# An attention and FP4-FFN layer on one core: the quantisation of the FFN weights is taken apart and its pieces are placed in the second pass

## The reference

```
xn   = (x - mean) / sqrt(var + 1e-5)
attn: q = xn @ Wqa @ Wqb (16 heads of 8), kv = xn @ Wkva @ Wkvb (4 kv heads of 8)
      rope on q and k, causal softmax(q k^T / sqrt(8)) v, @ Wout + bout
ffn:  gate = fp4(xn) @ fp4(w_gate)^T,  up = fp4(xn) @ fp4(w_up)^T     (352 hidden)
      h = silu(gate) * up,  out = fp4(h) @ fp4(w_down)^T
out  = x + attn + ffn
```

## Time and profile before

| | |
|---|---|
| runs (median) | 821.9 us |
| profiled execution | 822.47 us, its span 820.7 us, mean granted clock 0.969 |
| busy: PE, DVE, ACT, POOL | 91%, 78%, 67%, 73% of the span |
| chain that ended last | PE 73%, DVE 8%, ACT 6%, POOL 4%, SyncE's queue 3% |
| PEclk, 40 slices | `9668799999999999999999999999999999999997` |

### The profile page before, as it was taken

How to read it: one execution, slowest core, us unless ns; L and a number is a source line. 1 busy time by engine, 2 the same in 40 slices (tenths; PEclk the granted TensorE clock), 3 DMA queues, 4 the chain that set the end, 5 groups by cost and what they waited for, 6 DMA issues and landing times.

```text
span 820.7 us, 18663 instructions
## 1 busy us (share of the span) xinstructions
PE 746.0 (91%) x6641; PEld 468.1 (57%) x6733; DVE 637.2 (78%) x1396; ACT 553.2 (67%) x1169; POOL 602.6 (73%) x706
## 2 busy tenths in 40 slices
PE   2277899999999999999999999999999999999886
PEld 1143455665657565665756566666656565656444
DVE  4479788888788888888788888888887888787310
ACT  1213586777777777777777777777777777776771
POOL 5324597878879797878788797878788797856561
PEclk9668799999999999999999999999999999999997
DMA  4412323141314233241414232241413232230000
GB/s 115 124 48 77 78 75 80 54 107 50 86 45 112 58 93 76 58 111 45 98 36 109 53 105 64 63 106 50 111 49 84 47 97 60 81 75 9 21 15 14
DMA packets 66518, 58.24 MB, mean 71 GB/s; under 512 B 17554, under 2 KB 56434, under 8 KB 66426
## 3 DMA queue, kind: packets, MB, share of 16 engines
q1 hardware_dynamic: 66426, 57.04, 27.0%
HBM read 31.81 MB, written 18.61 MB: 61 GB/s over the span
## 4 chain that ended last, share of the span: by engine, by line
PE 73%; DVE 8%; ACT 6%; POOL 4%; SPq 3%; issue 3%; DMA 2%; another core or an unknown queue 0%; POOLq 0%; DVEq 0%; ACTq 0%
PE pv_ps L1038 18%; PE max_ps L1002 12%; PE exp_ps L1017 11%; PE misc_ps L1054 6%; PE max_ps L1003 6%; PE misc_ps L1103 5%; DVE neg_max L632 4%; PE misc_ps L1062 3%; PE misc_ps L1081 3%; ACT P L840 2%; PE misc_ps L1101 2%; PE misc_ps L1091 2%; PE misc_ps L1071 1%; POOL P L478 1%; PE misc_ps L1058 1%
## 5 line engine op out<-in xcount | busy, mean ns | idle before, releaser
L632 DVE TENSOR_REDUCE neg_max<-max_ps 128x1 f32<-128x512 f32 (+3 forms) x768 | 433.2, 593 | 105.2 <-PE max_ps L1003 103.6
L840 ACT ACTIVATE P<-exp_ps 128x512 f32<-128x512 f32 x512 | 293.5, 596 | 176.7 <-remote 95.5
L1017 PE MATMUL exp_ps<-Q,K 128*128 128x384 bf16 (+3 forms) x932 | 208.4, 292 | 7.5 <-ACT P L840 6.0
L1002 PE MATMUL max_ps<-K,Q 128*128 128x384 bf16 (+2 forms) x768 | 199.5, 278 | 17.2 <-DVE neg_max L632 7.0
L1003 PE MATMUL max_ps<-Kd,Q 128*128 128x128 bf16 x1024 | 190.6, 221 | 1.5 <-DVE neg_max L632 1.5
L478 POOL TENSOR_SCALAR_AFFINE_SELECT P<-P 128x512 f32<-128x512 f32 x256 | 161.7, 667 | 32.6 <-ACT P L843 32.6
L1038 PE MATMUL pv_ps<-P,V 128*32 128x512 f32 (+3 forms) x2048 | 164.2, 438 | 1.2 <-POOL P L478 0.8
L1002 PEld LDWEIGHTS max_ps<-K,Q 128*128 128x128 bf16 x768 | 75.2, 100 | 88.7 <-DVE neg_max L632 44.8
L1003 PEld LDWEIGHTS max_ps<-Kd,Q 128*128 128x128 bf16 x1024 | 99.4, 99 | 42.7 <-issue 22.8
L510 POOL TENSOR_TENSOR h<-gate_sb,up_half 128x352 f32<-128x352 f32 x64 | 59.6, 932 | 70.8 <-DVE gate_sb L645 70.8
L1017 PEld LDWEIGHTS exp_ps<-Q,K 128*128 128x128 bf16 x1024 | 82.4, 98 | 37.0 <-ACT P L840 14.3
(11 more groups left out here) (113 smaller groups left out, 1022.1 us busy)
## 6 DMA issues: line engine op xcount, KB each, us to landing
Q<-q_scr SPq DMA_DIRECT2D x64, 224.0 KB
q_scr<-q_split SPq DMA_DIRECT2D x16, 384.0 KB, 2.6
Kd<-K SPq DMA_DIRECT2D x64, 96.0 KB
x_in<-x SPq DMA_DIRECT2D x16, 256.0 KB, 5.3
q_scr<-q_split SPq DMA_DIRECT2D x16, 256.0 KB, 2.9
x_res<-x SPq DMA_DIRECT2D x16, 256.0 KB, 5.7
out<-y SPq DMA_DIRECT2D x32, 128.0 KB, 3.0
K<-k_scr SPq DMA_DIRECT2D x64, 48.0 KB
```

The lines of the kernel that those rows point to most:

```text
L632: nc.vector.tensor_reduce(neg_max[:, pr // 4, i, heads[0]:heads[0] + len(heads), pr % 4], max_ps[r % 3][:, 0:len(heads) * n].rearrange("p ...
L840: nc.scalar.activation(P[g % 2][:, hh + r % 2, col:col + 512], ps[:, :], ACT.Exp, scale=SCALE).then_inc(exp_done, 1)
L1002: nc.tensor.matmul(ps[:, col:col + d], Qt, Kt[:, half, g, 0:d], start=True, stop=True)
L1017: last = nc.tensor.matmul(exp_ps[n % 2][:, col:col + width], K[par][:, half, pr // 2, kb * 128:(kb + 1) * 128], Q[par][:, pr, kb * 128:S], ...
```

## The change

Each engine's list is changed, the arithmetic is not, except for who does it.

- VectorE: `quantize_weights` is cut into four functions. In the second pass (`T.t0 == FIRST_T + 1`) `weight_scales` stands behind x's magnitudes and ahead of q_cos; `weight_magnitudes` and `weight_values` behind k_sin and ahead of the statistics of batch 1; `store_weights` ahead of slot 5.
- GpSimd: w_raw x w_inv, behind parts 1 to 3 of x and ahead of q_rope. Its wait for the weights moves there.
- ScalarE: w_mag = w_raw x 2^22, behind the first split of k and ahead of the second split of q.
- TensorE: the transposes stand at slot 5, ahead of xqT; the rest of the old function, now `weights_stored`, still stands after the second pass.

```diff
@@ gpsimd, iteration @@
                     for part in (1, 2, 3):
                         quantize(T, 2, part, *xs)
+                if T.t0 == FIRST_T + 1:
+                    pool.wait_ge(weights_in, 16 * N_WEIGHTS)
+                    pool.wait_ge(w_step, 4)
+                    nc.gpsimd.tensor_tensor(blocks(w_raw[:, :]), blocks(w_raw[:, :]), spread(w_inv[:, :]), ALU.mult).then_inc(w_step, 1)
...
-            iterate(pool, iteration, lambda: pool.wait_ge(weights_in, 16 * N_WEIGHTS))
+            iterate(pool, iteration)
@@ vector @@
+            def weight_scales():
+                dve.wait_ge(weights_in, 16 * N_WEIGHTS)
+                dve.wait_ge(consts_set, 2)
+                nc.vector.tensor_reduce(w_max[:, :], blocks(w_raw[:, :]), AX.X, ALU.max, apply_absolute_value=True).then_inc(w_step, 1)
+                scales(dve.wait_ge, w_max[:, :], w_scale[:, :], w_inv[:, :], w_step)
+            def weight_magnitudes():
+                dve.wait_ge(w_step, 6)
+                magnitudes(lambda s, n: dve.wait_ge(s, 6 + n), w_mag[:, :], w_step)
+                dve.wait_ge(w_step, 8)
+                nc.vector.tensor_tensor(w_raw[:, :], w_raw[:, :], w_mag[:, :], ALU.add).then_inc(w_step, 1)
+            def weight_values():
+                dve.wait_ge(w_step, 9)
+                nc.vector.tensor_tensor(w_raw[:, :], w_raw[:, :], w_mag[:, :], ALU.subtract).then_inc(w_step, 1)
+                dve.wait_ge(w_step, 10)
+                nc.vector.tensor_tensor(blocks(w_raw[:, :]), blocks(w_raw[:, :]), spread(w_scale[:, :]), ALU.mult).then_inc(w_step, 1)
+            def store_weights():
+                dve.wait_ge(w_transposed, 1)
+                (the five copies to wguT and wdT)
...
                 reduces(0, 5)
+                first = T.t0 == FIRST_T + 1
+                if first:
+                    weight_scales()
...
                 reduces(2, 5)
+                if first:
+                    weight_magnitudes()
+                    weight_values()
                 reduces(3, 0)
...
                 reduces(4, 4, 5)
+                if first:
+                    store_weights()
                 reduces(5, 0, 1, 2)
...
-            def quantize_weights():   (all of the above in one piece, w_raw x w_inv and w_mag on VectorE too)
...
-            iterate(dve, iteration, quantize_weights)
+            iterate(dve, iteration)
@@ scalar, extra @@
+                if (slot, r) == (3, 2) and T.t0 == FIRST_T + 1:
+                    act.wait_ge(w_step, 5)
+                    nc.scalar.activation(w_mag[:, :], w_raw[:, :], ACT.Copy, scale=2.0 ** 22).then_inc(w_step, 1)
@@ tensor @@
                 last.then_inc(w_transposed, 1)
+
+            def weights_stored():
                 pe.wait_ge(w_ready, 5)
...
                 for slot in range(NPAIR):
+                    if slot == 5 and T.t0 == FIRST_T + 1:
+                        transpose_weights()
                     max_tile(T, slot, 0)
...
-            iterate(pe, iteration, transpose_weights)
+            iterate(pe, iteration, weights_stored)
```

More of the change, by code:

```diff
@@ L620, in magnitudes @@
                 nc.vector.tensor_scalar(mag, mag, 1.5 * 2.0 ** 22, None, ALU.max).then_inc(sem_, 1)
+            def weight_scales():
[15 more added lines that the diff above has]
+                dve.wait_ge(w_transposed, 1)
+                for n in range(2):
+                    nc.vector.tensor_copy(wguT[:, n, :], max_ps[n][:, 0:F]).then_inc(w_ready, 1)
+                for c, (_, cn) in enumerate(FC):
+                    nc.vector.tensor_copy(wdT[0:cn, c, :], exp_ps[0][0:cn, c * E:(c + 1) * E]).then_inc(w_ready, 1)
             def reduce_tile(T, pr, r):
@@ L792, in iteration @@
                 reduces(7, 3, 4, 5)
[L794 to L816, removed]
             for k in (K[0], K[1], Kd):
```

## The result

The changed kernel takes 814.96 us (median of 7 runs, 813.69 to 816.36) against 820.27 (7 runs, 818.67 to 822.25) for the kernel before: ratio 0.9933, 95% interval 0.9917 to 0.9949. That is 5.3 us less; 4.9 less had been forecast. Its profiled execution took 814.38 us, span 812.6, where before it was 822.47 and 820.7. So the two profiles differ by 8.1 us, clearly more than the medians. Where each part of this is has to be asked of the two traces.

What follows compares the result with a forecast made beforehand. The start-up's end was taken as bound by VectorE's weight block, then by Kd's landing: 42.6 + 0.7 = 43.3 against 48.28, 4.9 us won, giving 817.6 profiled and 817.0 median; range 814.5 to 820.6.

Steps and rivals of the forecast that it cites:

- What the block's removal is worth: Third pass's start: without the 13.4 us weight block, Kd's landing at 42.6 ends the wait, 5.7 us before 48.28.
- s, the delay of the q chain: Second pass: moved pieces delay what feeds Kd's transfer by 0.7 us: 0.5 at q_cos, 0.1 w_mag, 0.1 q's last split.
- The race at 17.8 us: Second pass: VectorE's w_scale slips in before GpSimd's subtraction, margin 0.06 us; if GpSimd is first, the delay is 1.5 us.
- The product on GpSimd: Second pass: w_raw x w_inv takes 2.06 to 2.1 us, hidden by q_rope's wait for q_sin.
- VectorE's slack: Second pass: batch 1's statistics run 5 us late, x_inv ends at 39.8 to 40.9, leaving 2 to 3 us slack.
- The lead is carried to the end: From the third pass's start on, the 4.9 us won are carried unchanged to the kernel's end.
- The second rival: Second pass: the hold between VectorE and GpSimd costs more, gain 2.9 to 4.0 us, time 818 to 819.1; chance 0.30.
- The third rival: Second pass: Kd's copy lands at 40 to 41.5, gain 6 to 8 us, time 814 to 816; chance 0.08.
- The fourth rival: Third pass's start: the clock's rise does not move forward, up to 2.4 us given back, 819.5; chance 0.07.
- The fifth: Second pass: VectorE waits before q_cos for late weights; slower than before if they land after 21.6 us; chance 0.05.
- The signs it named: Trace marks expected, such as first score matmul at about 43.3 behind Kd's DMA and fourth pass's Kd wait ending near 80.4.

Runs made afterwards that it cites:

- e8: Changed kernel with magnitudes and values behind batch 1's statistics, 100 idle TensorE products ahead of the third pass and 26 in the tail; 813.89 us.
- e4: Changed kernel with the second pass's load of x_in issued behind the second halves of K, Q and Kd; 815.85 us.
- e6: Changed kernel plus 26 small idle TensorE products ahead of the last pass's transposes and output jobs; 815.36 us.
- e7: Changed kernel plus 100 small idle TensorE products between the transposes' stores and the third pass; 813.66 us.
- e5: Changed kernel with the loads of w_gate and w_up issued behind the mask DMAs; 825.04 us (1 run).
- e1: Changed kernel without any piece of the weights' quantisation, transposes and stores of the raw weights kept; 815.05 us.
- e2: Changed kernel with the weight block in one piece on VectorE, behind k_sin in the second pass; 815.50 us.
- e3: Changed kernel with weight_magnitudes and weight_values behind v_stage instead of ahead of batch 1's statistics; 814.51 us.
- e9: Changed kernel with values behind batch 1's statistics, 26 idle products in the tail and 60 ahead of the third pass; 812.65 us.

## Why the prediction was right

- **What the block's removal is worth.** Forecast: not its 13.4 us but the 5.7 us up to the landing of Kd. Right: in every version but e8 it is that landing that ends the wait. Its size was off by 0.8: from issue to the first score matmul it took 7.2 us (36.77 to 43.96), not the 6.4 of the fourth pass. That duration is not a constant. With Kd issued at 36.76 to 36.79 in six executions (the changed kernel three times, e4, e6, e7), the start stood at 43.96 to 44.40, so 7.2 to 7.6 us behind the issue; in e5, issued at 45.05, it was 7.4. These seven have the changed kernel's order on VectorE in the second pass. In e1, e2, e3 and e9, which have another, it was 6.55 to 6.72, close to the forecast. So it goes with the version more than with chance, and not with the moment of issue: e2 issues at 36.89, later than the changed kernel. What makes the difference was not tried; of x_in's load behind it e4 shows no effect.
- **s, the delay of the q chain.** Forecast 0.7, measured 0.58 (27.43 to 28.01): 0.31 at q_cos (0.5 said), 0 by w_mag, which took 1.12 us and just fitted in (0.1 said), 0.30 by the hold on q's last split (0.1 said). The race at 17.8 us went as assumed in all three executions of the changed kernel: w_scale at 17.78 or 17.79, GpSimd's subtraction 0.05 us behind it.
- **The product on GpSimd**, 2.10 us, hidden: q_rope still waited 0.46 us for q_sin.
- **VectorE's slack.** Forecast x_inv's second end at 39.8 to 40.9; it was 38.9, as the values ended at 31.98, not 32.7.
- **The lead is carried to the end.** Forecast 4.9, measured 4.3 at the start, 4.2 at the last sum. The sum with its two terms put right, 0.12 less in s and 0.78 more in the landing, gives the start exactly: 4.98 + 0.12 - 0.78 = 4.32. "Unchanged" holds only to about 1 us, though. From the third pass's q_cos to the fourth's it took 38.7 to 39.5 us in three executions of the changed kernel and 38.9 and 39.8 in two of the kernel before; from there to the last sum all five agree within 0.45. Between the last sums of any two of them the lead is 3.4 to 5.5. Why the third pass varies was not tried.
- **The measured 5.3 us are therefore 1 us more than the mechanism gives.** I ascribe that to which runs had a slow tail and a long third pass; it is not shown, as only profiles tell. The three groups that had both kernels give 5.3, 7.1 and 3.9 us between the medians. Over all groups the kernel before has a median of 819.75 (58 runs) and the changed kernel 815.29 (21 runs), 4.5 us apart, and the lowest runs, 818.04 and 813.69, are 4.35 apart. So the forecast's 4.9 is too high by 0.6 for the mechanism, and that it comes close to 5.3 is in part luck.
- **The second rival** (the shared hold costs more) was there in kind: four VectorE and two GpSimd operations were stretched. But only 0.5 us of it lay on the path (0.2 at the last scale, 0.3 at q's split). The two-input half of the rule of the Trainium skill (page "SBUF — State Buffer", section "SBUF: two separate sides"), for which the prediction had no row, agrees with these traces: the addition of 1.32 us took 2.15 beside the splits; in e3, where it began ahead of rstd, it took 1.33 and rstd 2.10.
- **The third rival** (the transfer is earlier) did not happen: Kd landed at 43.82, not before 42.6.
- **The fourth rival** (the clock gives back up to 2.4 us) did not happen: the third pass's q_cos is 8.20 us behind its first matmul, 8.28 before. The granted clock was 0.50 at the start of that pass in both, and rose 5.4 us into it before and 5.2 after: the rise moved forward with the pass. e7 puts the price of the low clock at 1.8 us in the changed kernel.
- **The fifth** is shown by e5 to be real, with a break-even 0.8 us below the forecast's, but it was not near: w_max started at 16.43 with no wait.
- **The signs it named.** In the fourth pass the first score matmul is still released by Kd, at 81.24, where 80.4 had been said; but the chain goes by another matmul there, at 83.11 and behind the DMA of Q from m_row.
- **A slip in the range.** Its upper end, 820.6, is called the second's and fourth's, whose own times end at 819.1 and 819.5; nothing in the prediction leads to 820.6. It did not matter here.

Left open: what lets the clock fall in some tails and not in others. The three profiles with idle products in the tail have none slow, the nine of the changed kernel and its variants without have four, the kernel before two of two; that is a lean, not a proof. If the kernel before should have the slow tail more often than the changed one, part of the 5.3 us would be the change's after all; nothing here excludes that.

## What to carry to other kernels

Before a block on the path is moved, look for what it hides: the gain is the distance to the next wait, found here in a later pass where the same transfer stands in the chain alone. Place the moved pieces by what stands on the path at that moment and not by which engine is idle: three engines or one made no difference to the time, and the only delays that reached q_scr's write were 0.3 us in front of q_cos and 0.3 at q's last split. And compare profiles by a mark before the tail (the last sum) as well as by the span; here the tail alone differs by 2.6 us between two executions of the changed kernel, and by 3.9 between the first two profiles.

## What was not expected of the hardware

- GpSimd and VectorE hold each other even for tiny operations: rstd on 128 x 4 took 2.10 instead of 1.05 us beside a VectorE operation of two SBUF inputs, and one of VectorE's of 0.2 us waited 0.2 more.
- They alternate: VectorE's addition (27.01) waited for q's split, then k's split waited for the addition, then the subtraction for k's split.
- The duration of one and the same transfer, Kd's 192 KB, ranges over 0.4 us between executions of one kernel issued at the same moment (7.2 to 7.6 from issue to use), and is 6.55 to 6.72 in four other versions. Moving the 256 KB load of x_in from behind it changed nothing that can be seen (7.2).
- In e9 sixty idle products ran from 37.9 to 41.4 and the third pass started at 2.4 GHz, even with 1.75 us of idle time between; its q_cos came 1.8 us sooner behind its start. Without them, in the changed kernel, the clock had fallen by 39.0.
